# Graph network on one core: picked groups spaced five apart, one comparison for the one-hot rows, one comparison per line

## What is computed

```python
# layer 0: relational attention, per edge e = (src, dst, etype)
x_ = h[src]; y_ = h[dst]; c = w_comp[etype]
msg   = einsum('eb,ebo->eo', c, einsum('ei,bio->ebo', x_, weight))
a     = tanh(relu(sum((x_ @ A1_w.T + A1_b) * (y_ @ A2_w.T + A2_b + rel_emb[etype]), -1) / sqrt(32)))
nei   = segment_sum(a[:, None] * msg, dst)      # + h[src of the last edge of a node] @ self_loop_weight
# layer 1: segment_sum(x[src], dst)
# layer 2: softmax over the edges of a node, then a weighted segment_sum
# layer 3: ten steps of f = 0.9 * dst_norm * segment_sum((f * src_norm)[src], dst) + 0.1 * feat0
```

## Time and profile before

| | |
|---|---|
| median of 3 runs | 1260.72 us |
| the profiled execution's own time | 1265.35 us |
| its span, first to last instruction | 1263.6 us |
| busy in the span: PE / DVE / ACT / POOL | 77% / 81% / 50% / 55% |
| mean granted TensorE clock | 0.778 of full |

### The profile page before, as it was taken

One profiled execution on the slowest core, in us unless ns is written; L12 is line 12 of the kernel. 1 busy time (PEld: TensorE's weight loads), 2 busy tenths in 40 slices (PEclk: granted clock), 3 DMA queues, 4 the chain that ended last, 5 costly groups with the idle time before them and its releaser, 6 DMA issues.

```text
span 1263.6 us, 58393 instructions
## 1 busy us (share of the span) xinstructions
PE 977.7 (77%) x23808; PEld 898.6 (71%) x23808; DVE 1020.9 (81%) x3443; ACT 638.0 (50%) x1731; POOL 698.4 (55%) x686
## 2 busy tenths in 40 slices
PE   2368788788788787787788677767827995999996
PEld 2357677677677676676677566666726995999996
DVE  8679999889888988898889888888844997655556
ACT  1146666656565555565566555555688980000000
POOL 5777777777777777777777777777600000000000
PEclk9557777777777767767777777767758997999998
DMA  4522222122222221122122212221100000000001
GB/s 108 73 46 56 51 46 46 46 48 48 47 46 46 46 45 45 45 46 45 45 46 46 44 46 45 45 45 41 18 14 3 3 4 3 4 4 4 4 4 18
DMA packets 55896, 46.32 MB, mean 37 GB/s; under 512 B 37442, under 2 KB 51837, under 8 KB 55624
## 3 DMA queue, kind: packets, MB, share of 16 engines
q1 hardware_dynamic: 34056, 31.45, 8.9%
q0 software_dynamic: 21568, 11.09, 6.9%
HBM read 40.19 MB, written 2.28 MB: 34 GB/s over the span
## 4 chain that ended last, share of the span: by engine, by line
PE 25%; DMA 21%; DVE 17%; issue 14%; SPq 11%; POOL 10%; ACT 1%; DVEq 0%; POOLq 0%; ACTq 0%
PE ps L820 12%; POOL arena L587 10%; DMA arena<-line_table 10%; DMA agg_table<-arena 8%; PE ps L762 3%; SPq L519 3%; SPq L496 3%; PE ps L728 3%; DMA arena<-x_pad,arena 3%; DVE arena L1271 2%; SPq L520 2%; SPq L500 2%; DVE arena L1465 2%; DVE arena L1269 1%; PE ps L709 1%
## 5 line engine op out<-in xcount | busy, mean ns | idle before, releaser
L587 POOL DMA_INDIRECT arena<-x_pad,arena x674 | 696.5, 1033 | 205.8 <-issue 200.3
L728 PE MATMUL ps<-arena 128*32 128x44 f32 (+3 forms) x7832 | 204.9, 234 | 152.5 <-DVE arena L1300 152.1
L728 PEld LDWEIGHTS ps<-arena 128*32 128x32 f32 x7832 | 152.4, 133 | 192.7 <-DVE arena L1300 167.3
L1271 DVE TENSOR_SCALAR arena<-pair_no,arena 128x275 bf16<-128x275 f16 (+2 forms) x784 | 239.2, 308 | 0.0
L820 PE MATMUL ps<-arena,adj_words 128*128 128x64 f16 (+1 forms) x6250 | 195.7, 193 | 24.5 <-DVEq L1415 21.8
L820 PEld LDWEIGHTS ps<-arena,adj_words 128*128 128x128 fp8e4 x6250 | 193.5, 98 | 26.6 <-DVEq L1415 22.6
L1300 DVE TENSOR_TENSOR arena<-ps,arena 128x768 f32<-128x768 f32 x196 | 188.0, 959 | 6.7
L709 PE MATMUL ps<-arena 128*128 128x175 bf16 (+3 forms) x1567 | 164.0, 261 | 31.3 <-DVE arena L1271 30.4
L762 PE MATMUL ps<-aggT 128*128 128x128 bf16 x2268 | 175.3, 244 | 0.0
L1015 ACT ACTIVATE arena<-arena 128x4 f32<-128x4 f32 x196 | 40.2, 205 | 266.7 <-DVE arena L1286 255.9
L762 PEld LDWEIGHTS ps<-aggT 128*128 128x128 bf16 x2268 | 159.2, 112 | 0.0
(11 more groups left out here) (213 smaller groups left out, 1261.7 us busy)
## 6 DMA issues: line engine op xcount, KB each, us to landing
arena<-line_table SPq DMA_DIRECT2D x28, 602.0 KB
arena<-x_pad,arena POOLq DMA_INDIRECT x674, 3.3
arena<-line_table SPq DMA_DIRECT2D x28, 140.0 KB
arena<-pick_table SPq DMA_DIRECT2D x27, 128.0 KB
arena<-dst_parts SPq DMA_DIRECT2D x196, 5.7 KB
agg_table<-arena SPq DMA_DIRECT2D x196, 2.5 KB
dst_parts<-aggT SPq DMA_DIRECT2D x1, 735.0 KB, 14.7
x<-x_pad SPq DMA_DIRECT2D x1, 400.0 KB
```

What stands on the lines that cost most here:

```text
L587: pool.indirect_dma_start(to, None, table, bass.IndirectOffsetOnAxis(ap=index, axis=0)).then_inc(done, 16)
L728: return nc.tensor.matmul(to.rearrange("p (d m) -> p d m", m=MIX_COLS)[:, :, 0:m1 - m0], rows_of_slot, factors[:, :, m0:m1], start=False, ...
L1271: last = v.tensor_scalar(pair_hot[:, h, k, 0:n], pair_no[:, 0:n], pair_of[:, g, k:k + 1], None, ALU.is_equal)
```

## The change

The constants move, three pieces of code are replaced, and `make_rows` on ACT goes.

```diff
-LINE_AHEAD = 4
-PICK_AT, PICKS = LINE + 3, LINES - 1
-PICKED = range(PICK_AT, PICK_AT + PICKS * LINE, LINE)
+PICK_EVERY, PICK_LEAD = 5, 2
+PICK_AT = PICK_EVERY + PICK_LEAD
+PICKED = range(PICK_AT, GROUPS, PICK_EVERY)
+PICKS = len(PICKED)
-HOTS_AT = ((1, range(0, 4)), (2, range(4, PICK_DEEP)))
-ROWS_BY_SCALAR = 1
+HOTS_AT = ((0, range(0, 4)), (1, range(4, PICK_DEEP)))
+LINES_AT = LINE - 2
...
 # SP
                         if c >= 1:
                             load_lines(c)
-                        if c < PICKS:
-                            if c >= 2:
-                                sp.wait_ge(pick_hots, c - 1)
-                            sp.dma_start(codes[:, c % 2, :], ...)
+                    if g % PICK_EVERY == 0 and g // PICK_EVERY < PICKS:
+                        c = g // PICK_EVERY
+                        if c >= 2:
+                            sp.wait_ge(pick_hots, c - 1)
+                        sp.dma_start(codes[:, c % 2, :], ...)
...
 # ACT: make_rows and its calls are gone
-                    for k in range(ROWS_BY_SCALAR):
-                        last = a.activation(row_hot[:, h, k, :], row_no[:], ACT.Square, bias=row_f[:, g, k:k + 1], scale=-1.0)
...
-                    a.activation(hot_rows, hot_rows, ACT.Relu, bias=1.0, scale=-1.0).then_inc(row_hot_ready, 1)
...
 # DVE
-                def make_line(g):
+                def make_lines(c):
+                    dve.wait_ge(line_in[c % 2], 32 * (c // 2 + 1))
+                    own = lines[:, c % 2, :]
                     v.tensor_scalar(own, own, side_no[0:SIDE, 1:2], None, ALU.is_equal).then_inc(lines_ready, 1)
...
+                    n = [P, SLOTS, P // 2, 2]
+                    v.tensor_tensor(row_hot[:, h].rearrange("p k (v i) -> p k v i", i=2),
+                                    row_no[:].rearrange("p (v i) -> p v i", i=2).unsqueeze(1).to_broadcast(n),
+                                    row_twice[:, g].unsqueeze(2).to_broadcast(n), ALU.is_equal)
                     for k in range(SLOTS):
-                        if k >= ROWS_BY_SCALAR:
-                            v.tensor_scalar(row_hot[:, h, k, :], row_no[:], row_f[:, g, k:k + 1], None, ALU.is_equal)
...
-                    link(v.tensor_reduce(xp[:, PICKED[c] % AHEAD, :, 0:FEAT],
-                                         picked.rearrange("p (k w f) -> p k f w", k=SLOTS, w=PICK_WIDE), AX.X, ALU.add))
+                    of = picked.rearrange("p (k w f) -> p k w f", k=SLOTS, w=PICK_WIDE)
+                    half = PICK_WIDE // 2
+                    link(v.tensor_tensor(of[:, :, 0:half], of[:, :, 0:half], of[:, :, half:PICK_WIDE], ALU.add))
+                    link(v.tensor_tensor(xp[:, PICKED[c] % AHEAD, :, 0:FEAT], of[:, :, 0, :], of[:, :, 1, :], ALU.add))
...
                     score_edges(g)
                     if g + 1 < GROUPS:
                         make_pairs(g + 1)
-                    if g + LINE_AHEAD < GROUPS:
-                        make_line(g + LINE_AHEAD)
+                    if g % LINE == LINES_AT and g // LINE + 1 < LINES:
+                        make_lines(g // LINE + 1)
...
+                    if g % PICK_EVERY == 0 and 1 <= g // PICK_EVERY <= PICKS:
+                        read_picked(g // PICK_EVERY - 1)
                     for group, (at, _) in enumerate(HOTS_AT):
-                        if g % LINE == at and g // LINE < PICKS:
-                            make_pick_hots(g // LINE, group)
-                    if g % LINE == 0 and 1 <= g // LINE <= PICKS:
-                        read_picked(g // LINE - 1)
+                        if g % PICK_EVERY == at and g // PICK_EVERY < PICKS:
+                            make_pick_hots(g // PICK_EVERY, group)
```

More of the change, by code:

```diff
@@ L238, in gnn @@
         base_t = stay.cut(GROUPS + 1, I32)
-        row_f, pair_of, dst_off, last_off_1 = [stay.cut(GROUPS * SLOTS).rearrange("p (g k) -> p g k", k=SLOTS)
-                                            for _ in range(4)]
+        pair_of, dst_off, last_off_1 = [stay.cut(GROUPS * SLOTS).rearrange("p (g k) -> p g k", k=SLOTS) for _ in range(3)]
+        row_twice = stay.cut(2 * GROUPS * SLOTS, BF16).rearrange("p (g k i) -> p g k i", k=SLOTS, i=2)
         xp = stay.cut(AHEAD * SLOTS * SCORED).rearrange("p (u k c) -> p u k c", u=AHEAD, k=SLOTS)
@@ L509, in run_sweep @@
                             load_lines(c)
-                        if c < PICKS:
-                            if c >= 2:
-                                sp.wait_ge(pick_hots, c - 1)
-                            sp.dma_start(codes[:, c % 2, :], pick_table[c:c + 1, :].to_broadcast([P, WINDOW]))\
-                              .then_inc(code_in[c % 2], 16)
+                    if g % PICK_EVERY == 0 and g // PICK_EVERY < PICKS:
+                        c = g // PICK_EVERY
+                        if c >= 2:
+                            sp.wait_ge(pick_hots, c - 1)
+                        sp.dma_start(codes[:, c % 2, :], pick_table[c:c + 1, :].to_broadcast([P, WINDOW]))\
+                          .then_inc(code_in[c % 2], 16)
                     if g >= SIDES:
@@ L687, in fetch @@
                     c = g // LINE
-                    pe.wait_ge(lines_ready, g + 1)
+                    if g % LINE == 0:
+                        pe.wait_ge(lines_ready, c + 1)
                     pe.wait_ge(side_in[g % SIDES], 16 * (g // SIDES + 1))
@@ L774, in run_sweep @@
                         count(g + 1)
-                    if g // LINE < PICKS and g % LINE >= LINE - SLOTS:
-                        pick_tile(g // LINE, g % LINE - (LINE - SLOTS))
+                    if g // PICK_EVERY < PICKS and g % PICK_EVERY >= PICK_EVERY - SLOTS:
+                        pick_tile(g // PICK_EVERY, g % PICK_EVERY - (PICK_EVERY - SLOTS))
                     sum_mixed(g)
@@ L964, in run_sweep @@
                 act.wait_ge(sweep_cleared, 1)
-                def make_rows(g):
-                    h = g % 2
-                    if g >= 2:
-                        act.wait_ge(pairs_used, g - 1)
-                    for k in range(ROWS_BY_SCALAR):
-                        last = a.activation(row_hot[:, h, k, :], row_no[:], ACT.Square, bias=row_f[:, g, k:k + 1], scale=-1.0)
-                    last.then_inc(row_distances, 1)
-                    act.wait_ge(row_distances, g + 1)
-                    hot_rows = row_hot[:, h, 0:ROWS_BY_SCALAR].rearrange("p k v -> p (k v)")
-                    a.activation(hot_rows, hot_rows, ACT.Relu, bias=1.0, scale=-1.0).then_inc(row_hot_ready, 1)
                 def copy_counts(g):
@@ L1247, in run_sweep @@
                 dve.sem_inc(sweep_cleared, 1)
-                def make_line(g):
-                    c = g // LINE
-                    if g % LINE == 0:
-                        dve.wait_ge(line_in[c % 2], 32 * (c // 2 + 1))
-                    own = lines[:, c % 2, g % LINE * WINDOW:(g % LINE + 1) * WINDOW]
+                def make_lines(c):
+                    dve.wait_ge(line_in[c % 2], 32 * (c // 2 + 1))
+                    own = lines[:, c % 2, :]
                     v.tensor_scalar(own, own, side_no[0:SIDE, 1:2], None, ALU.is_equal).then_inc(lines_ready, 1)
@@ L1323, in read_picked @@
                     dve.sem_inc(pick_read, 1)
-                    link(v.tensor_reduce(xp[:, PICKED[c] % AHEAD, :, 0:FEAT],
-                                         picked.rearrange("p (k w f) -> p k f w", k=SLOTS, w=PICK_WIDE), AX.X, ALU.add))
-                for g in range(LINE_AHEAD):
-                    make_line(g)
+                    of = picked.rearrange("p (k w f) -> p k w f", k=SLOTS, w=PICK_WIDE)
+                    half = PICK_WIDE // 2
+                    link(v.tensor_tensor(of[:, :, 0:half], of[:, :, 0:half], of[:, :, half:PICK_WIDE], ALU.add))
+                    link(v.tensor_tensor(xp[:, PICKED[c] % AHEAD, :, 0:FEAT], of[:, :, 0, :], of[:, :, 1, :], ALU.add))
+                make_lines(0)
                 make_dst_hot(0)
@@ L1822 @@
         "x_pad": x_pad, "edges": edges,
-        "src_cols": columns(grouped[:, 0]), "pick_rows": grouped[:, 0].reshape(GROUPS, WINDOW)[PICK_AT::LINE][:PICKS], "dst_cols": columns(grouped[:, 1]), "next_cols": columns(after), "bases": bases,
+        "src_cols": columns(grouped[:, 0]), "pick_rows": grouped[:, 0].reshape(GROUPS, WINDOW)[PICK_AT::PICK_EVERY], "dst_cols": columns(grouped[:, 1]), "next_cols": columns(after), "bases": bases,
         "dst_rows_in": grouped[:, 1].reshape(LINE_ROWS, -1), "rel_rows_in": grouped[:, 2].reshape(LINE_ROWS, -1),
```

10 lines of the change are left out of this document (2 added, 8 removed).

## The result

The changed kernel takes 1245.74 us (median of 4 runs, 1243.25 to 1247.06), against 1260.99 us for the kernel before over 4 runs: the ratio is 0.9875, 95% interval [0.9855, 0.9894], some 15 us faster. The forecast gain was 5.8 us: the sign was right and the time lies in the recorded range, but the gain was undersized by more than half, and much of the error has a cause that the profile of before could have told.

The account below looks back on a forecast made before the run. SP's chain of line loads and stores, 149.05 to 929.18 us, was taken as the bound; -4 + 9.4 - 7.5 - 1.7 - 2 = -5.8 us on the median of 1260.7 gave 1254.9 us, range 1243 to 1268 us.

Parts of the forecast that it names:

- start, line 4 loaded: Up to line 4's load at 149.05 us, where DVE sets the pace: -4 us, bounds -10 and -1.
- codes between stores: On SP, 23 codes loads no longer hidden behind a line's load, at 0.41 us each: +9.4 us.
- block behind a line: From a line's load to SP's second store: 15 of 24 lose their codes, 0.5 us each, -7.5 us, bounds -7.5 and 0.
- late PE wait, and all other steps of SP: SP's waiting for PE's fetches late in the sweep goes: -1.7 us; nothing forecast for SP's other steps.
- from the last line to the sums: The 25 stores at the end wait 6.9 us for one another, partly behind gathers: -2 us, bounds -6.9 and 0.
- This chain of SP: SP's line loads and stores, held up behind each line's load, set the sweep's end; DVE and POOL close behind.
- The gathers at nothing: 44 fewer gathers on POOL, 59 us less there, hidden by SP's chain and so worth nothing but a lighter DMA load.
- the second rival: Codes loads between two stores hold up the next store: slower, up to 1278 us at 1 us each; chance 0.13.
- The third: Rival: PE becomes the bound, staying at its lower clock of 1.2 GHz: slower, +12 us, 1267 us; chance 0.06.
- The first rival: POOL's gathers were the bound: 59 us faster, 1202 us, or partly, 1225 us; chance 0.11.

Follow-up runs that it names:

- before_no_gathers: The kernel before without the gathers of groups 21 to 195 and without DVE's waits for them: 1238.61 us, ratio 0.9832.
- before_no_codes: The kernel before with only its first two loads of picked codes, the later ones left out: 1258.77 us, ratio 0.9986.
- before_picks: The kernel before with the change's picks alone (38 instead of 27, codes loaded apart from lines, two additions for the reduction): 1258.05 us, ratio 0.9983.
- before_rows_lines: The kernel before with the new row comparison and the lines compared at once, keeping its 27 picks and 674 gathers: 1247.69 us, ratio 0.9913.
- before_lines: The kernel before with only the comparison of a whole line at once, two groups later: 1249.92 us, ratio 0.9902.

## Why the prediction was wrong in size

In the traces the sums are loaded 22 us earlier. By the steps of the prediction, with the mean of the two traces of each kernel:

| step | forecast | measured |
|---|---|---|
| start, line 4 loaded | -4 | -7.4 |
| codes between stores | +9.4 | +7.8 |
| block behind a line | -7.5 | -11.5 |
| late PE wait, and all other steps of SP | -1.7 | -3.5 |
| from the last line to the sums | -2 | -7.3 |
| sum | -5.8 | -21.9 |

- **What bounds: half right, and this is the step that failed.** "This chain of SP, 149.05 to 929.18 us, ends the sweep", and the gathers' "POOL ends by 912 us, SP at 929 us: hidden" took the 17 us between as slack. They were the path of the last groups through DVE, PE, ACT and the last eight stores, the same 17 us in the four kernels whose last gather starts after 905 us. In the kernel before, both chains end together; SP's own would have needed 149 + 707 + 66 = 922 us, the gathers hold it to 929. The tail was therefore undersized, -2 where -7.3 was measured: of the 6.9 us in the earlier trace rows I took a third, because only part stood "behind gathers", yet without late gathers the whole stretch is 6 to 7 us shorter. How much of that is stores that land late and how much is sums that come late was not separated.
- **The gathers at nothing.** Right for the main part: 59 us of POOL's work went and SP's chain hid them, as before_no_gathers shows. Wrong for the last 6 to 7 us. And I counted only the gathers taken away: those that remained became faster as well, worth 630 x 0.030 = 19 us on POOL, and the lines alone bring the last gather forward by 26 us.
- **The start.** The parts were priced well: lines -7.0 and -2.1, measured -7.9 alone; rows between -4 and +2 (the recorded -0.5 to +0.2 us a group would be -10 to +4 for 20 groups), measured -1.1; picks +2.9, measured +0.8 alone and +2.5 on top of the others. Their sum near -7 was written down, and I then took -4 from fear of slow pick tiles on PE. The earlier trace rows shows such tiles, but no row showed anyone waiting for them.
- **The block behind a line.** The codes' 0.5 us a block is confirmed (before_no_codes 16.0, against 16.5 and 16.6). The count was one too high: 14 of the 24 blocks lose their codes, as line 27 had none before, so -7.0 us. The other 4 to 5 us come from a further 0.2 us in every block, with codes or without; before_picks has it, before_rows_lines has not. So it comes with the picks. That gathers delay the blocks is shown (0.8 us without any), but 6.5% fewer of them would explain 0.05 us; the rest stays open.
- **All other steps of SP.** Beside the 1.7 us, SP's short waits for PE's fetches before the side rows (line 519) fell from 7.3 to 4.9 us between line 4 and the last line: a term that the prediction had at nothing.
- **Codes between stores** cost 0.34 to 0.36 us for 0.41, and hold up nothing: the second rival is dead. The third too: the granted clock rose to 0.83 in the stretch of the earlier trace rows, PE is busy 78.90% there.
- **The first rival**, at 0.11, was nearer to the truth than that number says. It holds for the kernel before once SP's line load is repaired (DVE then waits 63.5 us for gathered rows), and as the kernel stands the gathers count at its end. That the time still lies in the recorded range is in part luck: the blocks' -11.5 and the tail's -7.3 us lie outside their own bounds (-7.5 and -6.9).
- POOL ended at 834 us, "tens of us before", as said, but it was not made to wait for PE: 3.4 us in all.

Some 3 to 7 us of the 21.9 are scatter of the executions profiled: the medians differ by 15.2 us and, in the second set of runs, by 18.7 us.

## What to carry to other kernels

When two chains end close together, the distance between their last instructions is not slack: subtract first what the last piece of work still has to pass through, and compare only what is left. A change that shortens one of two equal chains earns nothing, as repairing SP's line load alone (-2 us) or taking codes away alone (-2 us) shows; this change paid because it shortened both. A broadcast load is worth a look wherever a queue stands still behind it: 86 rows cost a 16 us block, 80 and 6 cost 7.7 us. And an engine off the chain can be slowed by the order of work on another: here gathers on POOL grew long where DVE's comparisons stood in one particular order.

## What the runs showed of the hardware

**A DVE comparison can hold a gather up.** The median gather is 945 to 947 ns in the kernels before, after and in each of the parts; only the share of long ones changes. Between 200 and 800 us, gathers above 1.1 us number 53 of 449 before and 31 of 460 after. What they meet on DVE decides. Before, 38 gathers meet comparisons for a pick (line 1312), which there always stand directly behind a line comparison (line 1254): all 38 are long, 1733 ns on average. Of the 106 that meet a line comparison but none for a pick, 13 are long; of the 305 that meet neither, 2. The long ones took 35 us more than the median in all, 30 of them in those 38. One of them, POOL and then DVE (the gathers before and behind it take 0.95 and 0.94 us):

```profile
489.26 2.18 POOL L587 DMA_INDIRECT arena<-x_pad,arena  x1 [0.30 <-issue]
```

```profile
489.92 0.35 DVE L1254 TENSOR_SCALAR arena<-arena,side_no 106x512 bf16<-106x512 bf16 x1
490.18 1.14 DVE L1312 TENSOR_SCALAR aggT<-arena,pick_no 128x512 bf16<-128x512 f16 x4
```

The comparisons for a pick do not do this by themselves. In before_rows_lines, where none stands behind a line comparison, 80 gathers meet them and none is long; in before_lines it is 4 of 56. In before_picks the three that still stand directly behind a line comparison make all 24 gathers long that meet them, the others 7 of 55; in the changed kernel it is 4 of 4 and 0 of 89. A whole line in one comparison (3584 columns) makes 20 of 28 gathers long, and the new two-tensor row comparison 5 of the 142 that meet it and no comparison of a line or pick. One of the changed kernel's meets both kinds:

```profile
463.56 2.65 POOL L588 DMA_INDIRECT arena<-x_pad,arena  x1 [0.30 <-issue]
```

```profile
463.21 1.16 DVE L1238 TENSOR_SCALAR arena<-arena,side_no 106x3584 bf16<-106x3584 bf16 x1 [1.88 <-DMA arena<-line_table]
464.28 0.87 DVE L1298 TENSOR_SCALAR aggT<-arena,pick_no 128x512 bf16<-128x512 f16 x3
```

So the lines at once do not make gathers faster (1033 to 995 ns on average) by holding DVE for 1.15 us where seven operations took 7 x 0.344 = 2.4 us. Of what the long gathers took above the median between 200 and 800 us, the part of those that meet a pick's comparisons falls from 30 us to 4 in before_lines, since these no longer stand behind a line comparison, while the rest rises from 5 to 13 us. The Trainium skill ("SBUF — State Buffer", SBUF: two separate sides and Who interferes with whom) says that a two-port operation of VectorE, which `tensor_scalar` can be and `tensor_tensor` cannot, locks GpSimd out of the ports with which it writes a DMA's descriptors. The trace agrees in that the two-tensor comparison makes few gathers long; by that rule the comparisons for picks should hold gathers up wherever they stand, yet the 80 gathers that meet them in before_rows_lines take 975 ns on average, against 1733 ns for the 38 of the kernel before. Why the order matters stays open, and no run tested the mechanism.

**A broadcast load to 86 rows.** Split into 80 and 6 rows, it lets the second store behind it go after 7.7 us instead of 16 us, and 28.05 us a line in the changed kernel instead of 30.42 us. The Trainium skill ("DMA: Bandwidth & Descriptors", How many engines) would put 86 rows on two DMA engines and 80 on sixteen; the direction and the size fit, and no trace here shows the engines one by one.

**A two-tensor comparison of 2-byte elements**, 128x512, takes 419 ns, and the 4-byte multiplication of the same size (line 1305) 678 ns. The Trainium skill ("VectorE: DVE Perf Modes", What auto-detection actually checks) lets a two-tensor operation on 2-byte elements reach two results a cycle; my estimate from that, half of 0.68 us or 0.34 us, is 0.08 us too low. Part of the 0.68 us does not halve with the rate: the 4-byte additions of 256 and 128 columns take 429 and 295 ns.
